# Four row tiles' lag maxima and exponentials grouped at one tile of an FFN, on one Trainium2 core

## The reference

```python
f = jnp.fft.rfft(xh, axis=-1)
corr = jnp.fft.irfft(f * jnp.conj(f), n=L, axis=-1)
top_k = int(FACTOR * math.log(L))                     # 6
weights, delay = jax.lax.top_k(corr, top_k)
tmp_corr = jax.nn.softmax(weights, axis=-1)
idx = (init_index + delay[..., None]) % L
pattern = jnp.take_along_axis(xh, idx, axis=-1)
delays_agg = jnp.sum(pattern * tmp_corr[..., None], axis=-2)
```

## Time and profile before

| | |
|---|---|
| median of 3 runs | 969.35 us (967.27 to 971.53) |
| span of the profiled execution | 966.3 us |
| the profiled execution's own time | not listed apart; the median lies 3.05 us above the span |
| PE busy | 782.0 us (81%) |
| DVE busy | 579.3 us (60%) |
| ACT busy | 338.6 us (35%) |
| POOL busy | 261.6 us (27%) |

### The profile page before, as it was taken

The page is one execution under the profiler, slowest core; times in us unless marked ns, Lnnn a source line. Parts: engine busy times, 40 slices in busy tenths (PEclk is TensorE's granted clock), DMA queues, the critical chain, the costliest instruction groups (busy, mean ns, idle before and its releaser), DMA issues.

```text
span 966.3 us, 14696 instructions
## 1 busy us (share of the span) xinstructions
PE 782.0 (81%) x4174; PEld 317.3 (33%) x4174; DVE 579.3 (60%) x1433; ACT 338.6 (35%) x544; POOL 261.6 (27%) x248
## 2 busy tenths in 40 slices
PE   1957667988998989887499926998757799999993
PEld 1622222222322322223244412453323344444441
DVE  7524776767677677004999998136999815722004
ACT  1122225655556456760033301447203322212220
POOL 3024452121212202321034412434301114323221
PEclk9978558999889999997889967999978899999997
DMA  9498988612312124522206667103997400201001
GB/s 267 84 194 283 263 243 205 114 27 47 67 29 45 38 48 100 94 56 79 44 13 171 200 107 218 56 1 73 149 215 148 80 9 0 44 1 44 0 1 43
DMA packets 144473, 94.16 MB, mean 97 GB/s; under 512 B 110184, under 2 KB 123368, under 8 KB 144216
## 3 DMA queue, kind: packets, MB, share of 16 engines
q1 hardware_dynamic: 133376, 71.24, 33.4%
q10 hardware_dynamic: 10816, 16.91, 5.6%
q0 software_dynamic: 240, 5.51, 2.7%
HBM read 49.51 MB, written 29.04 MB: 81 GB/s over the span
## 4 chain that ended last, share of the span: by engine, by line
PE 54%; DVE 16%; DMA 10%; issue 8%; SPq 5%; ACT 3%; POOL 2%; DVEq 0%; ACTq 0%; POOLq 0%
PE ps L1077 19%; PE ps L1089 8%; PE ps L1353 8%; PE ps L1321 7%; PE ps L1330 5%; PE ps L1063 5%; DVE mx L1237 3%; DMA lorad_d<-arena 2%; DMA lora_d<-arena 2%; SPq L334 2%; DMA qp_d<-arena 1%; DMA arena<-arena 1%; DVE arena L1233 1%; DVE stats L460 1%; DVE arena L500 1%
## 5 line engine op out<-in xcount | busy, mean ns | idle before, releaser
L1077 PE MATMUL ps<-arena 128*128 128x512 f16 (+1 forms) x976 | 224.7, 388 | 40.4 <-issue 22.6
L1300 ACT ACTIVATE arena<-ps 128x1024 f32<-128x1024 f32 (+7 forms) x256 | 163.4, 651 | 116.4 <-PE ps L1330 111.6
L1321 PE MATMUL ps<-arena 96*128 (+4 forms) x384 | 135.0, 377 | 37.9 <-DVE mx L1237 16.5
L1233 DVE CUSTOM_DVE_ANT_0 arena<-ps,arena 128x256 bf16<-128x256 f32 (+3 forms) x256 | 122.0, 488 | 58.1 <-PE ps L1321 50.0
L924 POOL TENSOR_TENSOR arena<-arena (+2 forms) x50 | 67.4, 1349 | 307.3 <-ACT arena L856 299.5
L1077 PEld LDWEIGHTS ps<-arena 128*128 (+2 forms) x976 | 97.7, 101 | 161.2 <-issue 54.2
L1330 PE MATMUL ps<-arena 99*128 (+4 forms) x384 | 125.7, 344 | 4.6 <-ACT arena L1300 4.2
L1089 PE MATMUL ps<-arena 128*128 (+3 forms) x488 | 114.6, 384 | 11.3 <-POOL arena L929 10.9
L1237 DVE TENSOR_REDUCE mx<-ps 128x1 f32<-128x512 f32 x128 | 88.2, 689 | 27.2 <-PE ps L1321 26.3
L1353 PE MATMUL ps<-arena 128*32 128x256 f32 (+1 forms) x1280 | 100.4, 387 | 2.8 <-POOL arena L1208 2.2
L1208 POOL TENSOR_SCALAR_AFFINE_SELECT arena<-arena 128x512 f32<-128x512 f32 x64 | 40.7, 635 | 225.5 <-ACT arena L1300 225.2
(11 more groups left out here) (144 smaller groups left out, 735.7 us busy)
## 6 DMA issues: line engine op xcount, KB each, us to landing
arena<-qp_d SPq DMA_DIRECT2D x48, 128.0 KB, 4.4
lora_d<-arena ACTq DMA_DIRECT2D x20, 256.0 KB, 4.7
arena<-lora_d SPq DMA_DIRECT2D x10, 512.0 KB, 4.2
w1n_d<-arena SPq DMA_DIRECT2D x10, 512.0 KB, 3.1
arena<-rec_d SPq DMA_DIRECT2D x32, 128.0 KB, 2.6
qp_d<-arena SPq DMA_DIRECT2D x12, 256.0 KB, 4.1
w1dn_d<-arena SPq DMA_DIRECT2D x4, 704.0 KB, 3.2
arena<-in_L_ffn_down_w_dram ACTq DMA_DIRECT2D x16, 172.0 KB, 3.4
```

The source lines that it names most:

```text
L1077: last = nc.tensor.matmul(ps[0:h, 2 * (n % 2) + o, :], w(t[0])[:, kt, bass.ds(ht * P, h)], xt[:, c, t[1], kt, :], start=(kt, t) == (0, ter ...
L1233: nc.vector.tensor_tensor_reduce(out=junk[:, h, 0:w], in0=s_bank(g, u)[:, 0:w], in1=strip[:, D - w:D], scale=1.0, scalar=3.0 * NEG, op0=AL ...
L1300: nc.scalar.activation(probs[:, kt % 2, h, kt * P:T], st_bank(h).rearrange("p b n -> p (b n)")[:, kt * P:T], ACT.Exp, scale=HD ** -0.5).th ...
L1321: nc.tensor.matmul(s_bank(g, u)[:, 0:k1 - k0], qt6[0:QROWS, g % RING, h, qt * P:(qt + 1) * P], kt6[0:QROWS, g, k0:k1], start=True, stop=Tr ...
```

## The change

The eight maxima of each row tile get a place of their own in `top` and `ntop`. DVE finds a row tile's maxima right after copying its correlations; the marking and the selection of all four row tiles come behind that. ACT does the four row tiles' exponentials together, at FFN tile 8, and writes the wide ones into `y` itself, where the selection then works in place; `expc` and the semaphore `pick_done` are gone. The functions are shared, so the second chunk's lag terms change in the same way, at the place where they were.

```diff
-        expc = room(176, [2, D])
...
-        x_done, pick_done = sem("x_done"), sem("pick_done")
+        x_done = sem("x_done")
...
-        top = sb("top", [P, 8])
-        ntop = sb("ntop", [P, 2])
+        top = sb("top", [P, SUB, 8])
+        ntop = sb("ntop", [P, SUB])
...
         def top_lags(dve, link, c, i):
 
             n = SUB * c + i
-            cr = corr[c][:, i, :]
-            if n > 0:
-                dve.wait_ge(e_ready, n)
-            link(nc.vector.max(out=top[:, :], in_=cr[:, 0:D]))
-            link(nc.vector.tensor_scalar(ntop[:, 0:1], top[:, 0:1], -1.0, None, ALU.mult))
-            nc.vector.memset(top[:, TOPK:8], SENT).then_inc(top_ready, 1)
+            if c:
+                dve.wait_ge(e_ready, SUB * c)
+            link(nc.vector.max(out=top[:, i, :], in_=corr[c][:, i, 0:D]))
+            link(nc.vector.tensor_scalar(ntop[:, i:i + 1], top[:, i, 0:1], -1.0, None, ALU.mult))
+            nc.vector.memset(top[:, i, TOPK:8], SENT).then_inc(top_ready, 1)
             dve.wait_ge(top_ready, n + 1)
-            link(nc.vector.match_replace(out=picked[:, :], in_to_replace=top[:, :], in_values=cr, imm_value=PICKED))
+
+        def pick_lags(dve, link, c, i):
+
+            n = SUB * c + i
+            link(nc.vector.match_replace(out=picked[:, :], in_to_replace=top[:, i, :], in_values=corr[c][:, i, :], imm_value=PICKED))
             dve.wait_ge(e_ready, n + 1)
-            nc.vector.scalar_tensor_tensor(out=y[:, i, :], in0=picked[:, 0:D], scalar=PICKED, in1=expc[:, i % 2, :],
-                                           op0=ALU.is_equal, op1=ALU.mult).then_inc(pick_done, 1)
-            dve.wait_ge(pick_done, n + 1)
+            link(nc.vector.scalar_tensor_tensor(out=y[:, i, :], in0=picked[:, 0:D], scalar=PICKED, in1=y[:, i, :],
+                                                op0=ALU.is_equal, op1=ALU.mult))
...
                 for i in range(SUB):
                     correlations(dve, link, c, i)
+                    top_lags(dve, link, c, i)
                 for i in range(SUB):
-                    top_lags(dve, link, c, i)
+                    pick_lags(dve, link, c, i)
...
             act.wait_ge(act_chain, k + 1)
-            if k >= 2:
-                act.wait_ge(pick_done, k - 1)
-            nc.scalar.activation(expc[:, i % 2, :], corr[c][:, i, 0:D], ACT.Exp, bias=ntop[:, 0:1]).then_inc(e_ready, 1)
+            nc.scalar.activation(y[:, i, :], corr[c][:, i, 0:D], ACT.Exp, bias=ntop[:, i:i + 1]).then_inc(e_ready, 1)
...
                     {AT0["rows"]: first_spectrum, AT0["spectrum"]: lambda: weight_spectrum(act, 0),
-                     **{AT0["lags"] + i: lambda i=i: lag_terms(act, 0, i) for i in range(SUB)}})
+                     AT0["lags"]: lambda: [lag_terms(act, 0, i) for i in range(SUB)]})
```

More of the change, by code:

```diff
@@ L777, in lag_terms @@
             act.wait_ge(top_ready, k + 1)
-            nc.scalar.activation(etop[:, 0:TOPK], top[:, 0:TOPK], ACT.Exp, bias=ntop[:, 0:1],
+            nc.scalar.activation(etop[:, 0:TOPK], top[:, i, 0:TOPK], ACT.Exp, bias=ntop[:, i:i + 1],
                                  accum_out=wsum[:, k:k + 1]).then_inc(act_chain, 1)
             act.wait_ge(act_chain, k + 1)
-            if k >= 2:
-                act.wait_ge(pick_done, k - 1)
-            nc.scalar.activation(expc[:, i % 2, :], corr[c][:, i, 0:D], ACT.Exp, bias=ntop[:, 0:1]).then_inc(e_ready, 1)
+            nc.scalar.activation(y[:, i, :], corr[c][:, i, 0:D], ACT.Exp, bias=ntop[:, i:i + 1]).then_inc(e_ready, 1)
         act_chain = sem("act_chain")
```

## The result

| | before | with the change |
|---|---|---|
| median | 969.25 us (964.63 to 973.68, 8 runs) | 975.68 us (970.50 to 978.72, 8 runs) |
| ratio, 95% interval | | 1.0059 [1.0031, 1.0087] |
| the same kernel in a second comparison | 968.95 us | 973.84 us, 1.0039 [1.0003, 1.0076] |
| span of the profiled execution | 966.3 us | 973.6 us (its own time 975.37) |

A forecast was written before the change was run, and what follows sets the result against it. The start of the lag spectra bounds the kernel: 674.43 us before, 675.2 with ACT's burst and loop loads, 676.5 with POOL's share. That +2.1 gives span 968.4, plus 3.05 for the median: 971.4 us, range 968.4 to 974.5.

The forecast's parts named there:

- POOL beside DVE on the second pass: Behind hidden(10), POOL's ops overlap DVE's `prepare_down`: between 0 and 0.87 us lost, half taken.
- What bounds the kernel: The chain around the lag terms: the start of `weight_spectra`, 674.43 us before, moves everything behind it by the same amount.
- W: Start of PE's `weight_spectra` (lag spectra, L1063): 674.43 us before, forecast 676.5, +2.1, bounds +0.8 to +2.6.
- DVE's part: Lag rows: maxima end near 643.6, ahead of ACT's load; pieces start near 652.9, 12.1 us earlier; the DMA gate goes.
- ACT's burst: At tile 8, one load and four pairs delay the Silu 3.5 us; out_of(7) starts at 656.8 instead of 653.33.
- The loads in the loop: FFN tiles 8 to 12: a load between the wait for PE and Silu stalls PE 1.19 us every second tile.
- rival B: PE's clock falls after standing still 3.7 to 4.6 us ahead of out_of(7): +1.7 to +2.4 us, 973.5 us; chance 0.27.
- Rival A: Loads in the loop cost nothing: about 969.4 us, chance 0.10; outer form, burst absorbed too: 965.2 us, chance 0.03.
- Rival C: `prepare_down` beside the FFN's POOL ops costs 0.87 us more in each of three tiles: +3.9, 973.2 us; chance 0.05.
- The prediction's point between 3.11 and 4.69 us: Idle length of PE from which its clock falls: full after 3.11 us, at its lower level after 4.69.

The follow-up runs named there:

- e3: Changed kernel with ACT's exponentials two at tile 8, two at tile 10, the tile behind each written out; 0.9966 of the kernel before, 38.3 us from first correlation product to lag spectra.
- e4: Changed kernel with three row tiles' exponentials at tile 7, one at tile 8, tile 8 written out; ratio 0.9975 to the kernel before, stretch 38.1 us.
- e9: The kernel with three exponentials at tile 7 and one at tile 8, measured once more; ratio 0.9961 to the kernel before, stretch again 38.1 us.
- e2: Changed kernel with ACT's exponentials spread again, one row tile at each of tiles 8 to 11; ratio 1.0024 to the kernel before, stretch 40.5 us.
- e1: Changed kernel with ACT's tile 8 written out, so no table load stands in the loop; ratio 1.0027 to the kernel before, stretch 43.0 us.
- e5: Kernel without loads in the loop, plus DVE held ahead of `prepare_down` until PE has done out_of(9); ratio 0.9995 to the kernel before, stretch 43.9 us.
- e6: Changed kernel with three exponentials at tile 8, one at tile 9, both tiles written out; ratio 1.0017 to the kernel before, stretch 41.4 us.
- e8: The changed kernel itself, nothing altered, measured again; 973.84 us, ratio 1.0039 to the kernel before, stretch 44.65 us.

## Why the prediction was wrong, step by step

It forecast 971.4 us, 2.1 over before, in a range up to 974.5, and put 0.87 on a difference within 0.5%. Measured are 975.68 and a ratio of 1.0059: slower, just past the line, where it had put 0.10. Of the 4.3 us between forecast and measurement, 2.1 lie in the stretch (forecast 676.5 - 633.95 = 42.5 us, measured 44.7), and there the runs show which terms of the sum failed: POOL beside DVE on the second pass, and the clock, which the sum had at nothing. The rest, some 2 us, no profile puts down to the change.

- **What bounds the kernel** was right: W decides. Up to the second FFN's first matmul the rest moved by 0.5 us, and e3 and e4 gain what their W gains, within the intervals. That everything behind W moves by just as much holds only to some 3 us: from that matmul to the end it is 212.2 us in e4's profile and 209.8 in e9's, of the same kernel.
- **DVE's part** was right. Four maxima ended at 647.8 (9.4 us after the product's start; forecast 9.6), ahead of ACT's load; pieces began at 657.37 after 638.39, 19.0 us (forecast 652.9 - 633.95 = 19.0); the DMA wait went. What that is worth by itself no run shows: in e2 the pieces start as late as before and the DMA wait is back, and in e3 and e4, where both are gone, ACT's part differs too.
- **ACT's burst** was right in kind, 0.9 too large with POOL's share. out_of(7) came 12.4 us after hidden(8), forecast 13.2. The pairs follow each other after 1.04 us, not 1.16, since an Exp starts while the one before ends (651.89, against 651.26 + 0.72), which gave 0.3; and POOL's two ops lost 0.34 us there, not 0.87.
- **The loads in the loop**: right, 1.19 forecast; e1 gave 1.7 back, of which 1.3 are the load and the rest POOL's.
- **POOL beside DVE on the second pass** was mis-sized: I took 0.44, half of what a row showed, with 0.87 as the bound. It was 1.8 (product 1.73 for 1.26, low 2.50 for 1.16), so the wait at out_of(9) was 2.8 us and not 1.6. The row that I bounded it by came from DVE instructions on 512 elements; those of `prepare_down` are on 1376, and each of the two POOL ops can wait for what is left of one: product(10) lost 0.47 to L609, which ended at 672.14, low(9) 1.34 to L593. Their lengths, 1.59 and 1.65 us, stood in the timeline of DVE; one of them for each POOL op was the right bound.
- **The clock**, rival B, came true; it had 0.27, and the sum had the clock at nothing. Price: 1.5 us in the profiled execution, a little below the 1.7 to 2.4 of the rival. It fell in all four profiles with the wait of 3.5 us (the change twice, e1, e5). Forecast with B was 4.2 us over before, measured are 6.4 and, in the second comparison, 4.9.

So W is 2.1 us later than forecast: -0.9 for the burst, +1.5 for the clock, +1.4 for POOL, and 0.1 in gaps. That the stretch's 4.2 us are B's +4.2 is luck: the burst's share was too large and the price of the clock too, and POOL's too small. With these terms as measured the forecast is 973.5, inside the range; the range would have held the second comparison's 973.84 and missed the first by 1.2 us, less than the some 2 us that the stretch does not explain. Rival A was wrong as a whole: the load costs where the loop puts it, behind the wait for PE. The drain behind a load, which rival A had in its price of 2.66 us, does not show here either: load at 655.11, Silu at 656.40. Rival C named the cause of the third term, but priced it by three tiles at 0.87; it was one at 1.8.

The range was also too narrow at its upper end for a plain reason: it took 1 us for the spread of the median at its lower end and next to nothing at its upper one, where two comparisons of one kernel came out 1.8 us apart. And it left out sums of B and C as two mishaps together; B and a POOL term above its bound are what happened.

## What to carry to other kernels

Grouping activations by table saves loads only if the group fits into time in which nobody waits for that engine; a group in front of queued work delays all of it at once, where single ones spread out each hid almost wholly (0.3 to 0.4 us a tile in the kernel before). Look for the idle time just ahead, here the 8.7 us while PE did the correlation products. And look at what the grouping does to the generated loops: a loop whose entry has another table than its end carries a load in its body, behind the wait that it could have been hidden in front of; writing out one iteration takes it away.

For two engines that shut each other out, bound the collision by the longest single instruction of the other one that can stand there, once for each instruction that can meet one, and not by a collision seen with shorter ones.

## What the runs showed of the hardware

The clock of TensorE fell after shorter waits than the profile of before had shown. There it had stayed up after 2.56 and 3.11 us of idle and fallen after 4.69. In e6 it fell after 2.14 us, and ahead of a single place, the last down products of the first FFN, where every kernel here waits 2.56 us, it stayed up in five of eleven profiles and fell in six. The two forms, in the profile of before (the earlier trace rows have the clock's levels) and in that of the kernel after:

```profile
692.71 3.63 PE L1089 MATMUL ps<-arena 128*128 128x512 bf16 x16 [2.56 <-POOL arena L929]
```

```profile
701.35 5.31 PE L1089 MATMUL ps<-arena 128*128 128x512 bf16 x16 [2.57 <-POOL arena L929]
```

16 matmuls in 3.63 or in 5.31 us, at a granted clock of 1.00 (692.7 to 696.3) or 0.68 on average (701.3 to 706.7). At that place it costs nothing, as PE waits for POOL's L913 behind it either way (4.69 us of idle, or 3.00). The prediction's point between 3.11 and 4.69 us, and the length that it cites from the Trainium skill's TensorE: Matmul & The Clock Gate, HAM oscillation, are no safe limits here: the measurement decides. What decided it in each case stays open. After waits of 1.6 us and less it never fell in the stretch.

The row of 3.11 us, on which that point rested, was one outcome of two as well. Ahead of the second chunk's correlation products PE waits 3.1 to 3.4 us in every profile; the clock stayed up behind it in five (48 matmuls in 5.49 us) and fell in six (6.83 to 8.31). The kernel after did both, 7.15 us in its first profile and 5.49 in e8's, and so did that of e4 (5.49) and e9 (8.31). The line of the kernel after, in its first profile, beside the earlier trace rows; and then, from e3's profile (8.18 us at that place), the second FFN's first matmuls:

```profile
751.72 7.15 PE L1063 MATMUL ps<-arena 128*128 128x257 f16 x48 [3.19 <-POOL arena L906]
```

```profile
752.61 15.70 PE L1078 MATMUL ps<-arena 128*128 128x512 f16 x72 [1.81 <-DMA arena<-arena]
```

A fall at that place is not a loss, since PE waits for a DMA behind it; and where PE works longer there, that wait is shorter. In e3 and e9 it was 1.81 and 1.70 us, the clock was full from the second FFN's first matmul on, and its first 72 matmuls took 15.70 us; with waits of 2.4 to 5.1 us they took 17.39 to 18.57 in the other nine. The time from that matmul to the end goes with it: 209.8 us in those two, 211.5 to 212.6 in the others. So alike programs differ by up to 2.8 us behind the place of the change, by which way the clock went.
